# A selective-scan mixer: the product with B of the next state made ahead of the product with C of the last one

## The reference

```python
A = -jnp.exp(A_raw)
def step(h, inp):
    x_t, dlt, B_t, C_t = inp
    dA = jnp.exp(dlt[:, None, :] * A[None])
    h = dA * h + dlt[:, None, :] * B_t[:, :, None] * x_t[:, None, :]
    y_t = jnp.einsum('bn,bnd->bd', C_t, h) + D * x_t
    return (h, y_t)
```

## Time and profile before

| | |
|---|---|
| median of 3 runs | 3794.38 us (3793.55 to 3797.54) |
| the profiled execution | 3792.99 us |
| its span, first to last instruction | 3791.1 us |
| mean granted TensorE clock | 0.927 |
| mixer stage with the scans | 170 to 1575 us |
| 128 scans, mean of one | 566.0 us, 4422 ns |
| 128 `into`, mean of one, idle before | 292.8 us, 2287 ns, 87.2 us |
| 128 `out`, mean of one, idle before | 290.0 us, 2266 ns, 0.0 us |
| exponentials `dA`, idle before | 326.6 us, 129.0 us |

### The profile page before, as it was taken

The page is one execution under the profiler, slowest core; times in us unless marked ns, Lnnn a source line. Parts: engine busy times, 40 slices in busy tenths (PEclk is TensorE's granted clock), DMA queues, the critical chain, the costliest instruction groups (busy, mean ns, idle before and its releaser), DMA issues. The chain is left out here.

```text
span 3791.1 us, 40920 instructions
## 1 busy us (share of the span) xinstructions
PE 3210.4 (85%) x12812; PEld 1740.6 (46%) x12813; DVE 2149.7 (57%) x2698; ACT 1601.5 (42%) x3089; POOL 636.4 (17%) x767
## 2 busy tenths in 40 slices
PE   7787878778787863399979999999999999987996
PEld 5343433434252420166634444444444444445775
DVE  1398989888999988622214353535344444433334
ACT  3556566565656552133314242333324242323443
POOL 0000202020202020223300010110202020205772
PEclk8898989899898975599989999999999999998998
DMA  1344454536454455522130001010101010036557
GB/s 61 88 119 132 129 142 123 151 109 156 130 144 134 129 139 156 178 71 67 58 122 1 28 28 42 14 49 6 55 1 55 1 55 1 33 133 208 159 157 266
DMA packets 193227, 362.86 MB, mean 96 GB/s; under 512 B 28274, under 2 KB 85106, under 8 KB 191922
## 3 DMA queue, kind: packets, MB, share of 16 engines
q1 hardware_dynamic: 164514, 296.19, 27.4%
q0 software_dynamic: 20352, 57.17, 4.1%
q10 hardware_dynamic: 8208, 7.54, 0.6%
HBM read 250.53 MB, written 110.28 MB: 95 GB/s over the span
## 5 line engine op out<-in xcount | busy, mean ns | idle before, releaser
L1644 DVE TENSOR_TENSOR_SCAN hs<-dA,hs 128x2048 f32<-128x2048 f32 x128 | 566.0, 4422 | 7.1
L453 POOL COPY rows<-slot 128x64 f32<-128x64 f32 x48 | 17.4, 394 | 2728.2 <-DVE new_pl L590 2684.4
L2233 PE MATMUL ps<-pT,V 128*128 128x512 f32 x1024 | 450.7, 593 | 0.9 <-DVE pT L2401 0.9
L1484 ACT ACTIVATE dA<-dl,w_An 128x511 f32<-128x511 f32 x512 | 326.6, 711 | 129.0 <-DVE hs L1644 115.1
L1636 DVE TENSOR_TENSOR hs<-u,bb 128x2048 f32<-128x2048 f32 x128 | 292.8, 2287 | 87.2 <-issue 38.1
L1321 PE MATMUL ps<-hs,w_S 128*32 128x512 f32 x1024 | 160.5, 699 | 205.6 <-DVE hs L1650 205.6
L2233 PEld LDWEIGHTS ps<-pT,V 128*128 128x128 f32 x1024 | 189.6, 190 | 221.1 <-issue 214.8
L1650 DVE TENSOR_TENSOR hs<-hs,cb 128x2048 f32<-128x2048 f32 x128 | 290.0, 2266 | 0.0
L1803 POOL DMA_INDIRECT slots<-og,idt x232 | 241.8, 1042 | 260.2 <-DVE og L1891 197.7
L449 POOL DMA_INDIRECT sorted<-rows,new_pl x192 | 270.5, 1409 | 63.6 <-issue 44.8
L2308 ACT ACTIVATE pp<-ps,nm 128x512 f32<-128x512 f32 x256 | 172.3, 685 | 215.0 <-DVE nm L2384 215.0
(11 more groups left out here) (354 smaller groups left out, 5445.3 us busy)
## 6 DMA issues: line engine op xcount, KB each, us to landing
bb<-bcd SPq DMA_DIRECT2D x128, 256.0 KB
cb<-bcd SPq DMA_DIRECT2D x128, 256.0 KB
dl<-dld SPq DMA_DIRECT2D x128, 256.0 KB, 7.2
u<-ud SPq DMA_DIRECT2D x128, 256.0 KB, 7.9
xg<-sorted SPq DMA_DIRECT2D x232, 136.0 KB, 2.1
slots<-zeros SPq DMA_DIRECT2D x136, 128.0 KB, 7.7
qrg<-slots SPq DMA_DIRECT2D x32, 512.0 KB, 16.2
rg<-slots SPq DMA_DIRECT2D x32, 256.0 KB, 4.9
```

The lines of the kernel that those rows point to most:

```text
L1484: act.activation(m.dA[:, N % 2, q, 1:T], m.dl[:, G % 2, q, 1:T], ACT.Exp, scale=An[:, e, N % GROUP:N % GROUP + 1]).then_inc(s_da, 1)
L1644: dve.tensor_tensor_scan(state, m.dA[:, N % 2].rearrange("p j t -> p (j t)"), state, 0.0, ALU.mult, ALU.add).then_inc(s_h, 1)
L2233: ins = pe.matmul(ps[:, 6 + j, :], V[:, m, h * D + j * P:h * D + (j + 1) * P], pT[:, i % 2, h % 2, m, :], start=(h == 0 and m == 0), stop= ...
```

## The change

In the loop of VectorE, `into(N + 1)` moves from behind `out(N - 1)` to ahead of it. The order within a step is now scan(N), `into(N + 1)`, `out(N - 1)`, side tasks. Nothing else is edited: the functions, their waits and the programs of the other engines are the same.

```diff
                             scan(N)
                             if n == 8 and b + 1 < B:
                                 soma_gated(dve, c, b + 1)
+                            if N + 1 < last:
+                                into(N + 1)
                             if N:
                                 out(N - 1)
-                            if N + 1 < last:
-                                into(N + 1)
                             tasks(b, n)
                     out(last - 1)
                     gate(B - 1, JI - 1)
```

## The result

The changed kernel takes 3918.28 us (median of 4 runs, 3916.40 to 3923.24), against 3793.97 us before (4 runs, 3789.66 to 3797.54). The ratio is 1.033, with a 95% interval of 1.0312 to 1.0348. The forecast was 3890 us within 3850 to 3925: the direction and the mechanism held, and the size was 28 us short.

The account below looks back on a forecast made before the run. VectorE, busy 90% of the mixer stage, was taken as the bound, with `u` arriving just in time. Terms: 33 + 24 + 27 + 14 - 2 = 96 us on 3792.99, 3889, so 3890 us as median; range 3850 to 3925.

Parts of the forecast that it names:

- rival 3: More than forecast: `u` late after the index load (+23), nothing hidden at n = 11 (+9), TensorE adds 15; over 3925: 0.08.
- The bound: Mixer stage: 1405 of 3791 us, VectorE busy 1264.76 us of it (90%); the change can act only there.
- The gap it closes: Between `into` and scan: 0.20 us less a step, 8.71 for 8.91; 62 such pairs, 12.4 us at most.
- The landing of `u` stays tied to its `out`: `u` lands some 8.8 to 9.65 us after the `out` that releases it; room shrinks from 8.82 to 4.25 us.
- Rivals 1 and 2: 1: transfers in time, only gaps close, 3784 us, chance 0.03. 2: `u` lands sooner than now, under 3850, chance 0.10.
- Terms A, B, D: Added waits for `u`: A at n = 7, 33 us; B at n = 11, 24; D at n = 15, 14.
- term B: At n = 11: `u` stall delays TensorE's accumulation and ScalarE's chain to L984, whose wait hides the rest; 24 us.
- a wait at L984 "about as now": Sign of being right: VectorE's wait for ScalarE ahead of the step size product, 51.1 us before, stays about as now.
- Term C: n = 0 to 3 of sequences 1 to 7: B row late behind the index load, then `u`; 27 us.
- TensorE's accumulation, counted at 0: It frees the buffer of `into(N+1)`: seven waits of some 2 us, covered by L984, counted 0; uncovered 15.
- a sign of being wrong: TensorE as what ends the waits of `into` (L1636) would show the forecast wrong.
- term A: Eight steps with n = 7, "no side task near": `into` waits for `u`, 4.1 us each, 33 us.

Follow-up runs that it names:

- experiment 1: SyncE's quarters of `dl` and `u` moved ahead of its wait for `out(N-1)`: on the changed kernel 3808.04 us, on the old order 3777.58 us.
- experiment 2: Changed kernel with TensorE's product for the temporal gate moved to the end of its step 7, ahead of the accumulation: 3901.21 us, ratio 1.0281.
- experiment 3: Changed kernel with the 512 KB store of the mixer's result moved behind the B row of n = 4 in SyncE's list: 3922.8 us, ratio 1.0333.

## Why the prediction was right, and where its sum was short

The measured 3918 us lies in the forecast range with 7 us to spare, and that it does is in part luck. The room above 3890 was argued from three causes (rival 3: `u` late after the index load, nothing hidden at n = 11, waits for TensorE), and they are not what filled it: two costs, 36 us together, that stand nowhere in the prediction did.

- *The bound.* Right. VectorE's busy time didn't change (1264.76 and 1263.84 us), and all of the 127 us are waits between its instructions.
- *The gap it closes.* Right to the hundredth: 8.71 us for 8.91. The Trainium skill (VectorE: DVE Perf Modes, "The DRAIN you can't avoid") says of a row of copies that the semaphores between them cost nothing extra. It doesn't carry over to this pair, a 128x2048 product followed by a scan of its result: 0.20 us lie between a wait that ends with the instruction just before and one that was met long ago.
- *The landing of `u` stays tied to its `out`.* Right: 9.0 us after it in step 26 and 9.2 on average at n = 7 and 11, where 8.8 to 9.65 was read before. Moving the release (experiment 1) took the waits away, which shows the cause. Rivals 1 and 2 are out. The 2.6 us that follows from the Trainium skill's DMA: Bandwidth & Descriptors, "Anatomy of one DMA", is out for these loads too; that section gives its fit for DMAs that GpSimd issues, and SyncE issues these, so the prediction should not have applied it without saying so.
- *Terms A, B, D.* 33, 24 and 14 forecast; 30.3, 26.6 and 14.0 measured. In term B the reasoning held too: the wait at L984 fell from 51.1 to 30.8 us, so it did hide a part of n = 11. The sign that I gave for it, a wait at L984 "about as now", contradicted this reasoning and did not hold.
- *Term C.* 27 forecast, 20.4 measured. The B row of n = 2 didn't come 22.1 us after its C row but 21.2 in the second sequence, from the C row at 355.00 to `into(19)` at 376.15. Over the seven sequences it was 20.4 us on average, against 22.3 before: 13 us less in all. The `u` quarters of n = 3 came 9.6 us after their `out`, where I took 8.8, which gives 6 us back. The timelines of SyncE's queue and VectorE:

```profile
355.00 0.51 SPq L1059 DMA_DIRECT2D cb<-bcd  x1
...
368.51 0.60 SPq L1059 DMA_DIRECT2D bb<-bcd  x1
```

```profile
376.15 2.29 DVE L1636 TENSOR_TENSOR hs<-u,bb 128x2048 f32<-128x2048 f32 x1 [5.38 <-DMA bb<-bcd]
```

  The gate's 2.1 us at n = 0 was covered by that wait, as forecast.
- *TensorE's accumulation, counted at 0.* Right in the sum. `into` waits 16.3 us for it in all, nearly always at n = 13, ahead of L984. I had named TensorE ending waits of `into` as a sign of being wrong; it does so for 16.3 of 204.8 us. With `u` in time it is 21.9 us, in 13 places (experiment 1), nearly all at n = 11 and 13.
- *The step that failed* is in term A: "no side task near". I took the stall at n = 7 as ending with `out(6)`. But TensorE's accumulation of that state stands ahead of its side tasks of n = 8, and these feed a VectorE instruction that in the old order was never waited for. It is the same path that term B priced at n = 11, and I didn't follow it at n = 7: 23.6 us, removed to the last by experiment 2.
- *The second omission:* of SyncE's list I followed `u`, and the B row only at n = 2. At n = 4 two quarters of `dl` and the store of the result come to stand right ahead of a B row: 12.1 us at n = 5.

Those two are 36 us, of which the four terms' surplus of 7 takes a part: 96 - 7 + 36 + 2 for the gaps = 127.

What stays open: why the rest of the program, 2229 to 2244 us in these profiles, differs between kernels whose edits don't touch it.

## What to carry to other kernels

An operation that releases a transfer is not free to be moved behind one that waits for a transfer, even when neither depends on the other: look up, for each load in the queue, which instruction releases it and which uses it, and count what lies between in the new order. Here the closed gap was worth 0.2 us a step, and each load that had no slack cost some 4 us, net of that gap. A stall is priced only when each engine's queue behind the delayed instruction has been followed to the next place where somebody waits. And the transfers that arrive just in time are the thing to mend first: a few lines moved in SyncE's list made the old order 1.4% faster (ratio 0.986), which none of the orders of VectorE's instructions tried here did. The move in TensorE's list, which that kernel has too, gave the old order nothing: n = 8 takes 0.5 us more there than before, and the gain lies at n = 2, 3, 7 and 11.

## What the runs showed of the hardware

- A B row of 256 KB, issued at 785.80 right behind a 512 KB store and two quarters of `dl`, was there only at 798.83, 13.0 us later; the same kind of row for `into(19)` was there after 376.15 - 368.51 = 7.6 us. Taking either of the two from ahead of the row was enough. With the store behind it (experiment 3) the row went out at 786.80 and `into(54)` started without a wait at 798.10, 11.3 us later; with only the store ahead of it (experiment 1) this was 11.9 us (743.60 to 755.52). So neither of them alone made it 13.0 us late.
- The wait at n = 8 costs a second time, through TensorE's clock. Behind its 6.43 us of idling, the 8 matmuls of the temporal product took 5.54 us, 0.69 each. In experiment 2, where the same product runs ahead of such a pause, it took 3.69, and in the kernel before 3.70. The windows view gives the granted clock of the two places, 0.64 of the full 2.4 GHz (so for a part of the window the lower level, 1.2 GHz) and 1.00 (the column ahead of the DMA share):

```profile
829.00:838.00 9.00, 8.06 (x18) 2.69 (x19) 5.22 (x2) 1.31 (x2) 0.00 (x0) 0.64 0.43 101
```

```profile
812.00:817.00 5.00, 5.00 (x13) 2.21 (x13) 0.80 (x1) 4.26 (x7) 0.00 (x0) 1.00 0.37 94
```
